# One core, a token tower of circuit, attention and experts: the first batch's scores on two banks, and new orders for the first four batches

## The reference

```python
params = quantum_params[token_ids.reshape(-1)]            # 3 layers x 6 qubits x 2 angles
h = _circuit_expvals(params) @ post_w.T + post_b          # 6 expectation values -> 192 wide
n = _layernorm(h)                                         # attention, one head of 192
qkv = n @ W_qkv + b_qkv
h = h + softmax(q @ k.T / sqrt(192)) @ v
n = _layernorm(h)                                         # experts: 2 of 8 by gate score
p, idx = softmax(top_k(n @ Wg, 2))
y = gelu(n @ W1[e] + b1[e]) @ W2[e] + b2[e]               # 192 -> 384 -> 192
h = h + sum(p * y[idx])
```

## Time and profile before

| what | us |
|---|---|
| median of 3 runs | 286.31 (284.52, 286.31, 288.80) |
| the profiled execution, its own time | 288.43 |
| its span, from the first to the last instruction | 286.7 |
| busy in the span: PE / DVE / ACT / POOL | 209.2 / 171.9 / 120.8 / 200.2 |

### The profile page before, as it was taken

How to read it: one execution, slowest core, us unless ns; L and a number is a source line. 1 busy time by engine, 2 the same in 40 slices (tenths; PEclk the granted TensorE clock), 3 DMA queues, 4 the chain that set the end, 5 groups by cost and what they waited for, 6 DMA issues and landing times.

```text
span 286.7 us, 5700 instructions
## 1 busy us (share of the span) xinstructions
PE 209.2 (73%) x1559; PEld 149.3 (52%) x1559; DVE 171.9 (60%) x651; ACT 120.8 (42%) x293; POOL 200.2 (70%) x273
## 2 busy tenths in 40 slices
PE   0760599278877699698688899999999999992000
PEld 0550454123444244445446797787899998982000
DVE  5754899978797995856755586233477003532223
ACT  1001213454454332656446364655566676661000
POOL 5777787707992657477676777777777777777750
PEclk9999999755596755779656799999999999999555
DMA  7911001189900000000012211133333229985763
GB/s 152 297 24 14 4 3 13 13 322 363 322 8 1 9 13 14 9 14 14 13 39 52 56 37 27 43 99 90 102 89 92 76 75 328 351 247 165 237 223 117
DMA packets 26074, 29.85 MB, mean 104 GB/s; under 512 B 15162, under 2 KB 19889, under 8 KB 25851
## 3 DMA queue, kind: packets, MB, share of 16 engines
q1 hardware_dynamic: 19564, 21.54, 24.7%
q0 software_dynamic: 6480, 7.94, 9.2%
HBM read 14.13 MB, written 16.02 MB: 105 GB/s over the span
## 4 chain that ended last, share of the span: by engine, by line
PE 49%; DVE 23%; POOL 9%; issue 7%; ACT 5%; DMA 4%; DVEq 1%; POOLq 0%; ACTq 0%; SPq 0%
PE bank_b L2132 22%; PE bank_b L1886 6%; PE bank_a L2120 5%; POOL circuit L562 5%; PE bank_a L1893 4%; POOL shares_out L767 4%; PE bank_c L1905 3%; DVE nmax L1194 3%; ACT prob L1602 2%; DMA shares_out<-circuit,up 2%; PE bank_d L1844 2%; ACT keys_t L1580 1%; DVE circuit L881 1%; DVE form_s L1165 1%; DVE form_p L1161 1%
## 5 line engine op out<-in xcount | busy, mean ns | idle before, releaser
L767 POOL DMA_INDIRECT shares_out<-circuit,up x71 | 73.7, 1038 | 21.6 <-issue 16.8
L733 POOL DMA_INDIRECT routed<-rows,slot x64 | 62.5, 976 | 31.0 <-issue 16.5
L2132 PE MATMUL bank_b<-wide,up 128*128 x426 | 79.1, 336 | 1.7 <-issue 1.4
L2132 PEld LDWEIGHTS bank_b<-wide,up 128*128 128x128 f32 x426 | 68.9, 192 | 7.2 <-issue 5.5
L1765 ACT ACTIVATE circuit<-bank_b,up 128x192 f32<-128x192 f32 x71 | 29.9, 422 | 29.5 <-PE bank_b L2132 28.0
L562 POOL DMA_INDIRECT circuit<-angles,ids x32 | 31.7, 991 | 11.0 <-issue 9.1
L1753 ACT ACTIVATE up<-bank_a 128x384 f32<-128x384 f32 x71 | 34.3, 486 | 9.0 <-PE bank_a L2120 8.4
L1893 PE MATMUL bank_a<-keys_t,wt 32*128 32x512 f32 x64 | 27.4, 944 | 3.3 <-ACT keys_t L1580 1.9
L1886 PE MATMUL bank_b<-queries_t,keys_t 32*128 32x512 f32 x64 | 25.1, 866 | 4.9 <-ACT keys_t L1580 2.5
L1194 DVE TENSOR_REDUCE nmax<-bank_a 128x2 f32<-128x1024 f32 x16 | 19.5, 1219 | 9.3 <-PE bank_a L1893 9.3
L1602 ACT ACTIVATE prob<-bank_b 128x1024 f32<-128x1024 f32 x16 | 16.4, 1023 | 18.8 <-PE bank_b L1886 18.8
(11 more groups left out here) (438 smaller groups left out, 379.1 us busy)
## 6 DMA issues: line engine op xcount, KB each, us to landing
routed<-pad_rows SPq DMA_DIRECT2D x8, 528.0 KB, 5.3
out<-hres SPq DMA_DIRECT2D x7, 384.0 KB, 5.7
wide<-down_w SPq DMA_DIRECT2D x1, 2304.0 KB, 11.9
prob<-shares_out SPq DMA_DIRECT2D x3, 768.0 KB
up<-up_w SPq DMA_DIRECT2D x1, 1536.0 KB
angle_stages<-shares_out SPq DMA_DIRECT2D x2, 768.0 KB, 6.8
form_p<-shares_out SPq DMA_DIRECT2D x2, 768.0 KB, 6.8
up<-routed SPq DMA_DIRECT2D x71, 16.0 KB, 1.8
```

The source lines that it names most:

```text
L733: pool.indirect_dma_start(out=routed, out_offset=bass.IndirectOffsetOnAxis(slot[:, b, k, j:j + 1], 0), in_=rows[:, b, k, j, :], in_offset=None
L767: pool.indirect_dma_start(out=shares_out, out_offset=bass.IndirectOffsetOnAxis(xb[:, m, DEST:DEST + 1].bitcast(I32), 0), in_=y[:, m % RESU ...
L2132: mm = pe.matmul(bank_b[:, m % 2, 0:D], hid[:, m % STEP, c * P:(c + 1) * P], wide_flat[:, bass.ds(first + c * D, D)], start=(c == 0), stop ...
```

## The change

1. `score_bank` and `transposed_bank` give some score halves other PSUM banks, so that both halves of one batch can be in flight. `whole_scores(b)` issues all four plain score matmuls of batches 0, 1 and 4 in one go on four row groups, `whole_transposed(b)` all four transposed ones of batches 0 and 3. `crossed_scores(b, h)` does for batches 1 and 2 what `both_scores` did, and `scores_until` follows the order of the halves, which is 1, 0 for batches 2 and 3.
2. Batch 0's `context`, `variance2`, `route`, `slots` and `shares` stand ahead of other batches' steps in VectorE's list; `ranks(0)` runs once batch 0's own values are there (not batch 1's).
3. VectorE's, ScalarE's and TensorE's lists up to batch 5 are written anew. GpSimd's and SyncE's are unchanged. The loops over the later batches and the experts are unchanged.

```diff
+        def score_bank(b, h):
+            if (b, h) == (1, 0):
+                return bank_a[:, 2:4, :]
+            return bank_b[:, :, :] if (b, h) in ((0, 1), (1, 1), (4, 1)) else bank_a[:, 0:2, :]
+        def transposed_bank(b, h):
+            return bank_a[:, 0:2, :] if (b, h) in ((0, 1), (3, 1)) else bank_b[:, :, :]
+        def scores_until(b, h):
+            return 2 * b + (1 - h if b in (2, 3) else h) + 1
...
             def row_max(b, h):
-                dve.wait_ge(s_done, 2 * b + h + 1)
-                dve.tensor_reduce(nmax[:, b % 2, 2 * h:2 * h + 2], bank_a[:, 0:2, :], AX.X, ALU.max, negate=True
+                dve.wait_ge(s_done, scores_until(b, h))
+                dve.tensor_reduce(nmax[:, b % 2, 2 * h:2 * h + 2], score_bank(b, h), AX.X, ALU.max, negate=True
...
+            context(0)
             chain_link(1, 2)
+            variance2(0)
+            row_max(2, 1)
+            route(0)
             row_max(2, 0)
...
-                act.activation(prob[:, 2 * h:2 * h + 2, :], bank_b[:, :, :], ACT.Exp).then_inc(exp_done, 1)
+                act.activation(prob[:, 2 * h:2 * h + 2, :], transposed_bank(b, h), ACT.Exp).then_inc(exp_done, 1)
...
+            def whole_scores(b):
+                pe.wait_ge(keys_copied, b + 1)
+                pe.wait_ge(wt_copied, b + 1)
+                if b == 0:
+                    pe.wait_ge(up_copied, E)
+                if b == 1:
+                    pe.wait_ge(exp_done, 1)
+                if b == 4:
+                    pe.wait_ge(exp_done, 8)
+                for n in range(2):
+                    for h in range(2):
+                        scores(b, h, n)
+            def whole_transposed(b):
+                pe.wait_ge(queries_copied, b + 1)
+                pe.wait_ge(max_done, 2 * b + 2)
+                if b > 0:
+                    pe.wait_ge(exp_done, 2 * b)
+                for n in range(2):
+                    for h in range(2):
+                        transposed_scores(b, h, n)
+            def crossed_scores(b, h):
+                pe.wait_ge(queries_copied, b + 1)
+                pe.wait_ge(exp_done, 2 * b + h)
+                pe.wait_ge(keys_copied, b + 2)
+                pe.wait_ge(wt_copied, b + 2)
+                pe.wait_ge(max_done, 2 * b + 2 + h)
+                for n in range(2):
+                    transposed_scores(b, h, n)
+                    scores(b + 1, 1 - h, n)
...
-                pe.wait_ge(pu_done, b + 1 if b + 1 in CHUNK_START else min(b + 2, BATCHES))
+                pe.wait_ge(pu_done, b + 1 if b == 0 or b + 1 in CHUNK_START else min(b + 2, BATCHES))
...
+            whole_scores(0)
+            factor(1)
+            keys(1)
+            queries(0)
+            whole_transposed(0)
+            whole_scores(1)
+            context(0)
```

More of the change, by code:

```diff
@@ L1362, in _ @@
             chain_start(1)
+            chain_link(1, 1)
             row_max(1, 0)
-            chain_link(1, 1)
             row_max(1, 1)
             spread_max(1)
+            context(0)
             chain_link(1, 2)
+            variance2(0)
+            row_max(2, 1)
+            route(0)
             row_max(2, 0)
[L1369 to L1372, removed]
             spread_max(2)
[L1374 to L1378, removed]
             normed(0)
-            row_max(3, 1)
-            spread_max(3)
             slots(0)
             shares(0)
+            context(1)
+            chain_link(1, 3)
+            variance2(1)
+            row_max(3, 1)
+            route(1)
+            row_max(3, 0)
+            spread_max(3)
+            chain_link(1, 4)
+            normed(1)
+            chain_ends(1)
             chain_close(1)
+            context(2)
             both_ends(1)
             variance1(1)
-            context(2)
-            variance2(1)
+            variance2(2)
             form(1, 0, E)
             features(2)
-            route(1)
-            features(3)
-            normed(1)
             slots(1)
             shares(1)
-            variance2(2)
+            features(3)
+            context(3)
+            route(2)
+            normed(2)
+            variance2(3)
             row_max(4, 0)
-            route(2)
-            context(3)
             row_max(4, 1)
             spread_max(4)
-            row_max(5, 0)
-            normed(2)
-            variance2(3)
             slots(2)
             shares(2)
+            route(3)
+            row_max(5, 0)
+            normed(3)
+            slots(3)
             row_max(5, 1)
             spread_max(5)
-            route(3)
-            normed(3)
-            slots(3)
+            shares(3)
             row_max(6, 0)
-            shares(3)
             context(4)
@@ new lines, in both_scores, with scores, transposed_scores @@
+                    if 0 <= bs < BATCHES:
+                        scores(bs, 1 - h, n)
+            def scores(b, h, n):
+                j = 2 * h + n
+                r = slice(j * F, (j + 1) * F)
+                mm = pe.matmul(score_bank(b, h)[:, n, :], wt[r, b % 2, :], keys_t[r, b % 3, :], start=True, stop=True)
+                if n == 1:
+                    mm.then_inc(s_done, 1)
+            def transposed_scores(b, h, n):
+                k = 2 * h + n
+                r = slice(k * F, (k + 1) * F)
+                mm = pe.matmul(transposed_bank(b, h)[:, n, :], keys_t[r, b % 3, k * P:(k + 1) * P], queries_t[r, :],
+                               start=True, stop=True)
+                if n == 1:
+                    mm.then_inc(st_done, 1)
```

149 lines of the change are left out of this document (71 added, 78 removed).

## The result

The change makes the kernel slower: 300.92 us (299.17 to 301.69, 4 runs) against 287.1 (284.52 to 288.80), ratio 1.0475, 95% interval 1.0427 to 1.0524. The forecast was 295.4 us, with a range of 285 to 302. The span of the profiled execution grew from 286.7 to 299.2.

A forecast was written before the change was run, and what follows sets the result against it. The prediction took GpSimd's scatters, paced by batch 5's `shares`, to bound the kernel. Its terms +2.9, +0.3, +3.1 and +2.8 sum to +9.1 us on 288.43, 297.5, less 2.1: 295.4 us, own range 292 to 299, stated range 285 to 302.

The forecast's parts named there:

- What bounds: GpSimd's list after the experts sets the end, which moves with batch 5's `shares`, not with the first scatter.
- the sign of being right: In the changed profile, first scatter at 87 to 89 us, then a wait of some 7 us before batch 1's.
- First stretch: Up to the end of `features(2)`: more waits and work put in front, less a stall moved away, +2.9 us.
- I let it be full between 76 and 96 us: Assumed TensorE clock in the walk: full from 76 to 96 us, then low until batch 4 is under way.
- Second: From `features(2)` to the end of `row_max(4, 1)`: stays about as long, 11 against 10.6 us, +0.3.
- Third: From `row_max(4, 1)` to `both_scores(4, 5, 0)`: `slots(2)`, waiting `shares(2)` and `route(3)` ahead of `row_max(5, 0)`, +3.1 us.
- Fourth: From `both_scores(4, 5, 0)` to `both_scores(5, 6, 0)`: `slots(3)` and `shares(3)` wait ahead of `row_max` steps, +2.8 us.
- Sum: The four stretches up to `both_scores(5, 6, 0)` added up, with no slack at batch 5: +9.1 us.
- the forecast's last step: From the profiled execution's 297.5 us to 295.4, as that execution lay 2.1 us above the median.
- the low clock: Rival: TensorE at the lower clock level throughout the walk, +13 us, 299.4 us; chance 0.13.
- The faster rival: Wide banks save TensorE-VectorE round trips, and work put ahead lies in VectorE's waits: -6.6 us, 279.7 us; chance 0.11.
- The stalled product: VectorE's 16-element product moves away from a GpSimd product: -1.5 us; if the stall only moves, total 10.6 instead of 9.1.

The follow-up runs named there:

- warm: Changed kernel plus 49 unread identity transposes in TensorE's waits between 77 and 106 us: 296.06 us, ratio 1.0293 to the kernel before.
- max5: Changed kernel with `row_max(5, 0)` straight behind `spread_max(4)`, ahead of `slots(2)`, `shares(2)`, `route(3)`: 297.22 us, ratio 1.0335.
- ranks3: Changed kernel with `ranks(3)` behind `both_scores(4, 6, 1)`, `row_max(5, 1)` and `spread_max(5)` ahead of `normed(3)`, `slots(3)`, and `row_max(6, 0)` ahead of `shares(3)`: 299.31 us.
- both: Changed kernel with the moves of max5 and ranks3 together: 294.34 us, ratio 1.0204.
- var3: Changed kernel with `variance2(3)` behind `spread_max(4)` instead of ahead of `row_max(4, 0)`: 298.61 us, ratio 1.0361.
- w4: Kernel before with only batch 4's four scores in one go on two banks, steps between moved behind: 284.09 us, ratio 0.9890.
- late: Kernel before with only the changed kernel's VectorE and TensorE orders of the third and fourth stretch: 296.25 us, ratio 1.0311.
- slots1: Changed kernel with `slots(1)` ahead of `form` and `features(2)` in VectorE's list: 300.12 us, ratio 1.0439.
- four: Changed kernel with the moves of max5, ranks3, var3 and slots1 together: 290.51 us, ratio 1.0104.
- link2: Changed kernel with `chain_link(1, 2)` moved from behind `context(0)` to ahead of `row_max(1, 0)`: 301.38 us, ratio 1.0499.
- fourwarm: Changed kernel with the moves of four and link2 and the extra transposes of warm: 286.97 us, ratio 0.9978.

## Why the prediction was right, and where it was off

- *What bounds.* Right: the end follows batch 5, not the first scatter. Batch 0's scatters came at 86.59 (forecast 87.4, and 87 to 89 as the sign of being right) and gave nothing. The wait behind them was 11.39, not some 7: they were over earlier, and batch 1's `shares` came later, since the first stretch was longer than walked.
- *First stretch, forecast +2.9, measured 49.87 - 45.32 = +4.6.* The new wait ahead of `row_max(1, 0)` was 2.31 (2.4 forecast), and VectorE's busy time grew by 40.17 - 38.62 = 1.55 (2.9 - 1.5 = 1.4 forecast). The waits were mis-sized: 6.4 walked, 7.6 measured, 1.2 of the 1.7 us that are missing. The step that failed is "I let it be full between 76 and 96 us": the clock was at 0.50 from 82 us, after TensorE had waited for `ranks(0)`'s input and for `slots(0)`. warm brings the waits to 4.6. This profile even lies at the short end: in max5, ranks3, both and var3, which do the same up to there, the stretch is 51.2 to 51.5, with a wait of 2.8 ahead of `row_max(1, 0)` and with a stalled product (see below).
- *Second, forecast +0.3, measured +1.8.* The four scores in one go, with what stood between moved behind, can save 3.2 us (w4, 10.60 to 7.43). They were spent on `variance2(3)` ahead of `row_max(4, 0)` (2.3, var3), on `context(3)`, which held `factor(4)` 2.85 us behind `features(2)`, and on the clock.
- *Third, forecast +3.1, measured 8.28 - 5.16 = +3.1. Fourth, forecast +2.8, measured 12.95 - 9.65 = +3.3.* Right in place and mechanism, and in size but for 0.5 of the fourth; max5, ranks3, both and late show it from both sides.
- *Sum.* +9.1 forecast, +12.7 at `both_scores(5, 6, 0)`. Of the missing 3.6 us, 3.1 are in the first two terms and 0.5 in the fourth. Some 2 more are in the forecast's last step: it took 2.1 off, because the profiled execution before lay that much above its median, while the one after, 300.97, lies at its own. So 300.92 is outside the forecast's own 292 to 299, and inside the stated range only by the room kept for the low clock. That rival, with +13 and 299.4 us, had the better size; I gave it 0.13 against 0.50, since I took the clock from the rows before instead of asking which new waits of TensorE come ahead of it. What I said for it misreads a row: the stretch of 0.50 before, 100 to 118 us, is not where TensorE waits most, for it is busy 16.60 of 18 us there. (Two slips of 0.1, 11 - 10.6 as +0.3 and 286.31 + 13 as 299.4, change nothing.)
- *The faster rival.* It had a real mechanism, the saved round trips, but the waits at `shares(2)`, `slots(3)` and `shares(3)`, 3.18, 5.03 and 3.20 us, did not vanish. The rule of the Trainium skill ("Perfetto Trace Analysis", section on matmuls) that matmul groups rotate through different banks so that one is emptied while the next is filled agrees with w4, where the four scores went to two banks and the steps between were moved: 1.1%.
- *The stalled product.* It took 1.68 us in the earlier trace rows. In the profile of after, VectorE worked like this beside the same GpSimd product, GpSimd's timeline first:

```profile
79.13 1.70 POOL L719 TENSOR_TENSOR pair_e<-pair_e,turn 128x720 f32<-128x720 f32 x1
```

```profile
79.28 1.22 DVE L1206 TENSOR_REDUCE nmax<-bank_a 128x2 f32<-128x1024 f32 x1
80.53 0.34 DVE L1213 COPY w_rep<-nmax 128x16 f32<-128x16 f32 x1
```

A `row_max`, which has one input, from a PSUM bank, ran beside it at its usual 1.22, and the short copy behind it took 0.34 instead of 0.18. But that is how the operations happened to fall in this execution. In eight kernels whose list is the same there or nearly so (max5, ranks3, both, var3, slots1, four, link2, fourwarm) the sum of the two halves of `mask` in `route(0)` stood beside that product for 1.57 to 1.71 us, where it takes 0.19 elsewhere. In max5, GpSimd's timeline first, then VectorE's:

```profile
79.18 1.77 POOL L719 TENSOR_TENSOR pair_e<-pair_e,turn 128x720 f32<-128x720 f32 x1
```

```profile
79.42 1.57 DVE L1291 TENSOR_TENSOR both<-mask 128x32 bf16<-128x32 f32 x1
```

So the stall did move to another two-input operation, as the rule of the Trainium skill ("SBUF — State Buffer", summary of rules) has it: that sum was the second to issue, and it ended at 80.99, the GpSimd product at 80.95. Of the kernels with the lists of after, only after itself and warm escaped it. Of the 1.5 us taken off for the stall, 2.93 - 1.55 = 1.4 came back in the profile of after, but only 0.5 to 1.0 in max5, ranks3, both and var3, where VectorE's busy time up to `features(2)` is 40.54 to 41.08. That 9.1 was nearer than 10.6 on this term is therefore in part luck of the profiled execution; how after's other executions fell is not on record.

## What to carry to other kernels

In a list that is worked through in order, a step that waits holds back the step behind it, and the end pays where it hangs on that step: the order with the wait of 3.18 us cost 4.0 (max5), the one with 5.03 and 3.20 cost 2.8 (ranks3). Elsewhere a wait that is taken away comes back at the next step (slots1, link2). Put the short reduction for which another engine waits ahead of routing work whose inputs come from a third engine, and judge a new order by what stands ahead of that reduction at each place. Ask of a step that is hurried whether the end waits for it; here the first scatter came 7.5 us earlier and the end 12.5 later. When a change gives TensorE new waits, price the stretch behind them at the lower clock, not at the clock that the old trace shows there.

## What was not expected of the hardware

49 transposes that compute nothing, in the waits between 77 and 106 us, raised the granted clock from 0.50 to 0.86 between 82 and 106 us and took 0.018 off the ratio, though TensorE's busy time in that stretch rose only from 14.70 to 16.11 us of 24, with 171 recorded pieces instead of 113. Two waits of 1.67 and 1.94 us, with the small matmuls of `ranks(0)` between them, had stood ahead of 24 us at the lower level.
